# A new head and small moves in a turn of an attention kernel, with 74 products on TensorE that nobody reads

## What is computed

```python
# layer 0, per image: xf is (C, N)
q, k, v = Wq @ xf + bq, Wk @ xf + bk, Wv @ xf + bv      # q, k of 32 rows, v of 256
attn = softmax(q.T @ k, axis=-1)
x1 = gamma * (v @ attn.T) + xf
# layer 1
h = group_norm(x1, 32 groups, eps=1e-5)                  # with weight and bias per channel
q, k, v = q_w @ h + q_b, k_w @ h + k_b, v_w @ h + v_b   # all of 256 rows
attn = softmax(q.T @ k / 16, axis=-1)
y = x1 + proj_w @ (v @ attn.T) + proj_b
```

## Time and profile before

| | us |
|---|---|
| median of three runs | 840.06 |
| lowest and highest | 836.66, 841.46 |
| the profiled execution | 842.42 |
| its span | 840.6 |
| PE busy | 789.0 (94%) |
| DVE busy | 556.8 (66%) |
| ACT busy | 471.2 (56%) |
| POOL busy | 166.7 (20%) |
| mean granted clock of TensorE | 0.982 |

### The profile page before, as it was taken

The page is one execution under the profiler, slowest core; times in us unless marked ns, Lnnn a source line. Parts: engine busy times, 40 slices in busy tenths (PEclk is TensorE's granted clock), DMA queues, the critical chain, the costliest instruction groups (busy, mean ns, idle before and its releaser), DMA issues.

```text
span 840.6 us, 9682 instructions
## 1 busy us (share of the span) xinstructions
PE 789.0 (94%) x3756; PEld 645.5 (77%) x3756; DVE 556.8 (66%) x787; ACT 471.2 (56%) x609; POOL 166.7 (20%) x141
## 2 busy tenths in 40 slices
PE   5788887999999989999999999999999999999998
PEld 4567666888788777877778877888778788888786
DVE  5554675677758686676956777586865857385665
ACT  4755663557654576445854657545765457444343
POOL 3600233201310041103310034100421024102300
PEclk9879999899999999999999999999999999999999
DMA  7000001001100011000200002000100001000101
GB/s 225 0 1 2 1 0 51 1 1 40 62 1 1 1 51 51 1 1 1 83 19 1 1 0 101 1 1 1 50 1 1 2 1 50 1 1 1 50 1 51
DMA packets 10365, 18.98 MB, mean 23 GB/s; under 512 B 2128, under 2 KB 3920, under 8 KB 10320
## 3 DMA queue, kind: packets, MB, share of 16 engines
q1 hardware_dynamic: 10320, 18.36, 6.3%
HBM read 9.97 MB, written 8.39 MB: 22 GB/s over the span
## 4 chain that ended last, share of the span: by engine, by line
PE 70%; DVE 20%; ACT 7%; issue 2%; DMA 1%; SPq 0%; ACTq 0%; DVEq 0%
PE ring L524 22%; PE ring L526 21%; PE ring L525 21%; PE ring L534 3%; DVE pt_lo L946 3%; PE ring L544 2%; ACT prob L743 2%; DVE neg_raw L931 2%; DVE bn L989 2%; DVE x_lo L861 2%; DVE neg_max L929 2%; DVE pt_lo L949 1%; DVE h_lo L869 1%; ACT ring L764 1%; DVE res L982 1%
## 5 line engine op out<-in xcount | busy, mean ns | idle before, releaser
L524 PE MATMUL ring<-pt_hi,v_hi 128*128 128x512 f32 x512 | 204.1, 399 | 4.2 <-issue 2.0
L525 PE MATMUL ring<-pt_lo,v_hi 128*128 128x512 f32 x512 | 202.6, 396 | 0.0
L526 PE MATMUL ring<-pt_hi,v_lo 128*128 128x512 f32 x512 | 202.5, 395 | 0.0
L743 ACT ACTIVATE prob<-ring,neg_max 128x1024 f32<-128x1024 f32 x64 | 71.6, 1118 | 179.1 <-DVE neg_max L932 179.1
L931 DVE TENSOR_REDUCE neg_raw<-ring 128x1 f32<-128x1024 f32 x64 | 77.9, 1217 | 86.9 <-PE ring L526 86.9
L465 POOL TENSOR_TENSOR v_lo<-v_f,v_hi 128x512 fp32r<-128x512 f32 x32 | 42.9, 1341 | 440.8 <-ACT v_hi L781 440.8
L524 PEld LDWEIGHTS ring<-pt_hi,v_hi 128*128 128x128 f32 x512 | 97.5, 190 | 26.7 <-issue 3.8
L526 PEld LDWEIGHTS ring<-pt_hi,v_lo 128*128 128x128 f32 x512 | 97.6, 191 | 21.8
L525 PEld LDWEIGHTS ring<-pt_lo,v_hi 128*128 128x128 f32 x512 | 97.8, 191 | 19.3
L524 PE MATMUL ring<-h_hi,query_hi 128*128 128x512 f32 x256 | 101.2, 395 | 5.2 <-DVE spread L967 4.9
L929 DVE TENSOR_REDUCE neg_max<-ring 128x1 f32<-128x1024 f32 x64 | 77.7, 1221 | 42.0 <-PE ring L534 42.0
(11 more groups left out here) (118 smaller groups left out, 1234.5 us busy)
## 6 DMA issues: line engine op xcount, KB each, us to landing
...
```

Of the source, the lines that this page charges most:

```text
L524: mm(out, w_hi, m_hi, start=first, stop=False)
L525: mm(out, w_hi, m_lo, start=False, stop=False)
L526: return mm(out, w_lo, m_hi, start=False, stop=last)
L743: activation(prob[:, p % PROBS], ring[:, slot], ACT.Exp, bias=neg_max[:, k % 2:k % 2 + 1], accum_out=row_sum[:, k % 2:k % 2 + 1]).then_inc ...
```

## The change

1. **Products that nobody reads.** `keep_busy` multiplies a 128 x 128 float32 matrix of ones by itself into a place that is filled afresh later: 48 times at the very start (after the ones are there), 10 times ahead of the first keys tile, 16 times ahead of the first value product. 74 in all.
2. **New head.** The scores of image 0 are no longer broken up by the last two value projections, which come later. POOL splits the first two (ACT copies them to `v1_f` first), ahead of its split of image 1, which goes to `h_hi` and `h_lo` and waits for nothing of TensorE. DVE instead of ACT takes the weight products. A step "opening" gives ACT and DVE an order of their own for both projections of image 1 and the shift. The bias products move from step 5 to step 0 of the keys, beside value projection 2.
3. **Image 0's steps.** Scores of image 1 are `late` in every step instead of `early`; all keys go to one slot. The split of x of image 2 moves forward into steps 6 and 7, and its lo half from POOL to DVE.
4. **Image 1.** Statistics, both norms and the hidden rows a step later, with other hosts; both phases of layer 0 of images 0 and 1 are evacuated at once.
5. **A turn.** The first qk projection is late in step 0; in step 3 the second stands ahead of all banks; norms are in sides instead of late.

The diff, cut to its core:

```diff
-PLACE = {("qk", 1, 0): 0, ("qk", 1, 1): 3}
+PLACE = {("qk", 1, 0): 2, ("value0", 0, 2): 3, ("value0", 0, 3): 0, ("value0", 1, 0): 0, ("value0", 1, 1): 0}
...
-HOST = {("norm", 0, m): ("qk", 2, m) for m in range(2)}
+HOST = {("qk", 1, 1): ("qk", 1, 0), ("bias", 0, 0): ("value0", 0, 2),
+        ("norm", 0, 0): ("qk", 2, 1), ("norm", 0, 1): ("value0", 2, 0)}
...
 def first_image():
...
-    steps = [Step(slots=(0, 1, 2, 3)) for _ in range(2)]
-    steps += [Step(slots=(0, 1, 2)), Step()]
-    steps[0].sides = tiles("qk", 0, (0, 1)) + tiles("value0", 0, (0, 1))
-    steps[1].late = tiles("scores", 0, (0, 1, 2)) + tiles("value0", 0, (2,))
-    steps[1].late += tiles("scores", 0, (3,)) + tiles("value0", 0, (3,)) + tiles("scores", 0, (4,))
-    for m, k in enumerate((5, 6, 7)):
-        steps[2].late += tiles("weights", 0, (m,)) + tiles("scores", 0, (k,))
-    steps[2].log = steps[2].shifts = 0
-    steps[2].late += tiles("weights", 0, (3,))
-    steps[2].take_weights = True
-    steps[3].sides = tiles("qk", 1, (0,))
-    steps[3].late = tiles("shift", 0, (0,))
-    for k in range(TILES + 2):
-        step = Step(("keys", 0, k) if k < TILES else None, (0, 0, k - 2) if k >= 2 else None, 1)
-        if k == 0:
-            step.sides = tiles("qk", 1, (1,))
-        if k == 2:
-            step.late = tiles("scores", 1, (0,))
-        if 3 <= k <= 5:
-            step.early = tiles("scores", 1, (k - 2,))
-        if 6 <= k <= 8:
-            step.early = tiles("scores", 1, (k - 1,))
-        if k in (4, 6):
-            step.sides = tiles("value0", 1, (k // 2 - 2,))
-        steps.append(step)
-    steps[4 + 5].sides = tiles("bias", 0, (0,))
-    steps[4 + 5].late = tiles("scores", 1, (4,))
-    steps[4 + 8].early_log = 1
-    steps[4 + 8].sides = tiles("value0", 1, (2,))
-    steps[4 + 8].late = tiles("shift", 1, (0,))
-    steps[4 + 9].sides = tiles("keys", 1, (0,))
-    steps[4 + 9].late = tiles("value0", 1, (3,))
-    steps.append(Step(("keys", 1, 1)))
-    steps[-1].split_x = 2
-    return steps
+    start, scores, opening = Step(slots=(0, 1, 2, 3)), Step(slots=(0, 1, 2)), Step()
+    start.sides = tiles("qk", 0, (0, 1)) + tiles("value0", 0, (0, 1))
+    scores.late = tiles("scores", 0, (0, 1, 2))
+    for m in range(4):
+        scores.late += tiles("weights", 0, (m,)) + tiles("scores", 0, (3 + m,))
+    scores.late += tiles("scores", 0, (7,))
+    scores.take_weights = True
+    opening.opening = True
+    opening.sides = tiles("qk", 1, (0, 1)) + tiles("value0", 0, (2,))
+    opening.late = tiles("shift", 0, (0,))
+    steps = [Step(("keys", 0, k), (0, 0, k - 2) if k >= 2 else None) for k in range(TILES)]
+    steps[0].sides = tiles("bias", 0, (0,))
+    steps[0].rest = True
+    for k in range(7):
+        steps[k + 1].late = tiles("scores", 1, (k,))
+    steps[3].sides = tiles("value0", 0, (3,))
+    steps[4].sides = tiles("value0", 1, (0,))
+    steps[6].sides = tiles("value0", 1, (1,))
+    steps[6].split_x = steps[7].split_x_lo = 2
+    s8, s9, s10 = Step(None, (0, 0, 6)), Step(None, (0, 0, 7)), Step(("keys", 1, 1))
+    s8.early = tiles("scores", 1, (7,))
+    s8.early_log = 1
+    s8.late = tiles("value0", 1, (2,))
+    s9.sides = tiles("shift", 1, (0,))
+    s9.late = tiles("keys", 1, (0,)) + tiles("value0", 1, (3,))
+    return [start, scores, opening] + steps + [s8, s9, s10]
...
-    s3.statistics = 0
+    s4.statistics = 0
     s4.sides = tiles("qk", 2, (0,))
-    s4.late = tiles("norm", 0, (0,))
-    s5.sides = tiles("qk", 2, (1,))
-    s5.late = tiles("norm", 0, (1,))
+    s5.sides = tiles("qk", 2, (1,)) + tiles("norm", 0, (0,))
     s6.early = tiles("scores", 2, (0,))
-    s6.sides = tiles("value0", 2, (0,))
-    s6.hidden = s6.hidden_lo = 0
+    s6.sides = tiles("value0", 2, (0,)) + tiles("norm", 0, (1,))
+    s7.hidden = s7.hidden_lo = 0
...
     if has(i + 1):
-        steps[0].sides = tiles("qk", i + 1, (0,))
+        steps[0].late = tiles("qk", i + 1, (0,))
+        steps[3].banks_first = 0
         steps[3].sides = tiles("qk", i + 1, (1,))
...
         for m, s in enumerate((12, 13)):
-            steps[s].late = tiles("norm", i, (m,)) + steps[s].late
+            steps[s].sides += tiles("norm", i, (m,))
...
         if _k == TILES - 1:
-            if _layer == 0:
+            if _layer == 0 and _image >= 2:
                 STEPS[_n + 1].evacuate = (_layer, _image)
             else:
                 _step.evacuate_at_once = (_layer, _image)
...
+
+            return (h_hi, h_lo) if i == 1 else (x_hi, x_lo)
...
+            def first_values0():
+
+                for m in range(2):
+                    two = slice(2 * m, 2 * m + 2)
+                    pool.wait_ge(S["value0_taken"], m + 1)
+                    link(G.tensor_copy(v0_hi[:, two], v1_f[:, m]))
+                    G.tensor_tensor(v0_lo[:, two], v1_f[:, m], v0_hi[:, two].bitcast(F32),
+                                    ALU.subtract).then_inc(S["value0_first"], 1)
...
             small_things()
+            first_values0()
+            first_split_x()
+            bias_rows()
             pool.wait_ge(S["x0_loaded"], 16)
             pool.wait_ge(x_loaded[0], x_loads(0))
             residual0(0)
-            first_split_x()
-            bias_rows()
             split_weights()
-            split_x(2)
...
+            def keep_busy(out, passes):
+
+                for _ in range(passes):
+                    mm(out[:, 0:P], ones[:], ones[:], start=True, stop=True)
...
+            wait("ones_ready", 1)
+            keep_busy(ring[:, 3], 48)
             for now in STEPS:
-                if now.tile:
+                if now.tile == ("keys", 0, 0):
+                    wait_read(BEFORE[now.tile])
+                    keep_busy(ring[:, SLOT[now.tile]], 10)
+                if now.values == (0, 0, 0):
+                    fill(now.tile)
+                    wait_read(BEFORE[0, 0, 2])
+                    keep_busy(pv_ps[:, 0], 16)
+                elif now.tile:
                     fill(now.tile)
...
+                    got = out[:, 0:HALF].rearrange("p (j n) -> p j n", j=2)
+                    if i == 0 and m < 2:
+                        copy(v1_f[:, m], got).then_inc(S["value0_taken"], 1)
+                    else:
+                        copy(v0_hi[:, 2 * m:2 * m + 2], got).then_inc(S["value0_hi"], 1)
...
+            def opening():
+                log_sums(0)
+                for m in range(2):
+                    query_part(("qk", 1, m))
+                shift_rows(("shift", 0, 0))
+                key_part(("qk", 1, 0))
...
+                if now.rest:
+                    key_part(("qk", 1, 1))
+                    project_hi(("value0", 0, 2))
...
+            def take_weights():
+
+                dve.wait_ge(S["ring_ready"], RING_NO["weights", 0, 3] + 1)
+                wqq_ps, wpv_ps = weight_places(SLOT["weights", 0, 3])
+                V.tensor_scalar(wqq_f, wqq_ps, scale, None, ALU.mult).then_inc(S["weights_read"], 1)
+                V.tensor_copy(wpv_f, wpv_ps).then_inc(S["weights_read"], 1)
+
+            def opening():
+                key_part(("qk", 1, 0))
+                shifts(0)
+                key_part(("qk", 1, 1))
+                for m in range(2):
+                    query_part(("qk", 1, m))
...
+                if now.rest:
+                    project_lo(("value0", 0, 2))
+                    project_lo(("bias", 0, 0))
```

135 lines of the change are left out of this document (74 added, 61 removed).

## The result

| | before | changed |
|---|---|---|
| median of the runs beside each other | 840.76 us (836.66 to 841.80, 4 runs) | 849.54 us (847.36 to 849.95, 4 runs) |
| the profiled execution, its span | 842.42 us, 840.6 | 847.36 us, 845.6 |
| the same in a later session (the last experiment) | 841.4 us (23 runs) | 848.86 us (6 runs) |
| TensorE busy in the span | 94% | 95% |

The changed kernel takes 1.0093 times as long, 95% interval 1.0063 to 1.0124, and in the second session 1.0103, 1.0075 to 1.013. It is slower by some 8 us, outside the predicted range. Of the 8.8 us between the medians the two profiled executions show 4.9: the one of before is the slowest of its first five runs, the changed one the fastest of its own.

What follows compares the result with a forecast made beforehand. TensorE, busy 94%, bounds the kernel, with a head where PE, ScalarE and VectorE take turns. Terms -0.2 + 2.8 - 3.3 - 6.2 + 4.1 + 3.0 = +0.2 on 842.42 give 842.6, or 840 us against the median; range 830 to 847.

Steps and rivals of the forecast that it cites:

- The 48 products and the first scores: Head: products end at 13.7 us (14.7 if the clock rises late), first scores at 20.1 instead of 16.65, loss 3.5.
- Rival A: Head: products at half price end before 8.86 us, head 4.8 + 1.1 us earlier, about 834 us; chance 0.14.
- gain 0.2: Scores of image 0: first keys at 36.3 us against 36.54, the new order's nearly 5 us taken by the products.
- the shift (0.6): End of image 0's scores: DVE's shift operations, after weight products and two key rows, take 0.6 us.
- loss 2.8: Rest of image 0, up to keys (1,2): these start at 98.1 us, where before it was 95.49.
- The loop of ScalarE and VectorE: Image 0's key steps: exponents, hi, lo and maximum close a loop of 5.7 us a step; PE isn't the limit.
- exp(3): Image 0's loop: ScalarE's exponent of keys 3, predicted at 52.4 us; PE waits for it at the value projection.
- The 16 products ... I cost at nothing: Ahead of the first value product, 42.5 to 46.1 us: covered by a later wait, cost nothing; up to 3.6 otherwise.
- loss 3 (0 to 6): PE's idle stretches between 50 and 120 us: two to three clock falls on the chain, some 1.3 us each.
- gains of 3.3 and 6.2: Image 1: first query projection 33.4 us after keys (1,2) instead of 36.7; at-once evacuation brings first logits 6.2 earlier.
- loss 4.1: Steady turns: DVE idles 0.8 us more in each of 5 turns, PE's wait moving to keys 2 for q.
- Rival C: Image 0, steps 2 to 7: ACT and DVE's exchange bounds, with a cold PE inside; about 847 us; chance 0.16.

Runs made afterwards that it cites:

- e10: e8 plus the 48 unread products ahead of everything, in the old head: 839.84 us, ratio 0.9981 to the kernel before.
- e8: Kernel before with only layer 0 of images 0 and 1 evacuated at once: 835.2 us, ratio 0.9925 to the kernel before.
- e5: Changed kernel with the turn's moves undone and GpSimd's residual0(0) and split_weights behind the shift: 842.07 us, ratio 0.9995 to the kernel before.
- e6: e5 without the 48 products during the loads: 838.8 us, ratio 0.9959 to the kernel before.
- e3: Changed kernel with GpSimd starting residual0(0) and split_weights only after VectorE's shift pair is written: 844.72 us, ratio 1.004 to the kernel before.
- e15: Changed kernel without any edit, timed again beside the kernel before: 848.86 us, ratio 1.0103.
- e11: e5 without any of the 74 unread products: 836.35 us, ratio 0.994 to the kernel before.
- e7: e5 without the 16 products ahead of the first value product: 841.56 us, ratio 0.9995 to the kernel before.
- e14: e5 without the 10 products ahead of the first keys: 841.49 us, ratio 1.0015 to the kernel before.
- e4: Kernel before with the turn's moves alone: 845.51 us, ratio 1.0042 to the kernel before.
- e12: Kernel before with the turn's moves except the group sums, which stay where they were: 845.92 us, ratio 1.0053 to the kernel before.
- e2: Changed kernel with the turn's moves undone, head, products and evacuation kept: 844.05 us, ratio 1.0031 to the kernel before.

## Why the prediction was wrong

Its structure held nearly everywhere; the time came out wrong by terms that were missing or set to nothing. Point by point:

- **The 48 products and the first scores.** Predicted to end at 13.7, with the scores at 20.1; measured 13.58 and 19.87. Right in this profile; in the second they end at 14.71 and the scores come at 21.00, which is the late rise of the prediction's bound (14.7), for which it had no row. Alone they cost 4.7 us (e10 over e8) and 3.0 us (e5 over e6), against a predicted net of 3.5. Rival A, half the price, is out: the 20 records from 36.53 to the keys at 38.74 start 0.11 us apart, so a product takes 0.22, as counted. The Trainium skill (TensorE: Matmul & The Clock Gate, "Wait — 56ns, not 53.3ns?") gives 55.6 ns at full clock for 128 columns; one record of a float32 product takes twice that here, and there are two.
- **First keys, "gain 0.2": wrong by 2.4.** The step that failed is "the shift (0.6)" in the part on the scores of image 0. VectorE's three operations took 2.9 us, since residual0(0) and split_weights of GpSimd had been moved to just this place. I followed VectorE's, ScalarE's and TensorE's queues, didn't follow GpSimd's past this place, and took the 0.17 us from a moment in which GpSimd idled. Without the overlap the first keys came at 36.36 (e3), against a predicted 36.3, and the whole was 4.5 to 5.3 us faster: 2.4 directly, the rest by the clock in that profile. In the second profile (e15) the first keys are 5.2 us later than predicted: 0.9 up to the first scores, 2.7 up to the shift, and 1.6 because the 10 products ran at a low clock.
- **The rest of image 0, "loss 2.8".** The loop of ScalarE and VectorE is right: in e11, without products, the value projection of step 3 starts 17.2 us behind the first keys (32.35 to 49.53), and the prediction's exp(3) ended 17.2 us behind them. From that projection to keys (1,2) the prediction has 44.6 us and e3 shows 44.4. "The 16 products ... I cost at nothing" held only where they ran at full clock. In e5 they take 3.74 us, near the predicted 3.6, and the distance of 17.2 us is the same with them as without them in e7. In the changed kernel they take 5.37 us, with a clock of 0.56 from 45.0 to 48.0 us, and the distance is 18.45 (in e3 4.73 and 18.3). They delay the scores behind them, which the loop needs. So this term was short by 1.3 us, and the clock made it so.
- **The clock, "loss 3 (0 to 6)".** About right, but it isn't one number. The last stretch took 44.4 us in e3 and e14, 46.0 in e5, 47.1 in the changed kernel and 47.5 in e11: 2.7 us in the changed kernel. In image 1 the first query projection came 34.5 us behind keys (1,2) (104.33 to 138.85), against a predicted 33.4; but it took 34.1 us in e5 too, at a clock of 1.00. So 0.4 of these 1.1 us are the clock's, and 0.7 were counted too short.
- **Image 1 and the evacuation, gains of 3.3 and 6.2.** Predicted 47.1 us from keys (1,2) to the first logits, measured 48.45 (48.1 in e5 at a clock of 1.00), before 56.64. The evacuation alone gave 6.3 (e8). Right but for 1.3 us: the 1.1 just named and 0.2 behind the first query projection.
- **The turns, "loss 4.1".** 0.82 us a turn, with the waits named and VectorE idle for 0.77 where 0.8 was predicted; 3.5 and 4.5 us in e4 and e12. Right.

In the profiled executions the misses (2.4 for the shift, 1.3 for the 16 products, 0.7 in image 1, 0.1 of clock) add up to 4.5 of the 4.8 us by which 847.36 exceeds the 842.6 of the sum. The rest of the distance to the medians is the spread of the head that e15 shows, and that the medians of before, 840.06 and 840.76, lay low in a kernel whose runs go from 836.8 to 843.2 in the last session. That the clock's 3 us came out so close is in part luck: in e3 and e14 the last stretch lost nothing.

One reading ahead of the sum was off, with no term resting on it: the page's digits are almost all 9 from slice 8 on, not from slice 6, and slice 7 reads 7. Rival C, at 847, had the right sign and a part of the mechanism (a cold TensorE in image 0, the 16 products uncovered), but not the cause in the head.

The parts add up. In distances of ratios times 842: turn +3.5 to 4.5, evacuation -6.3, the 48 products +3.0 to 4.7, the 10 and 16 together +1.6, GpSimd beside the shift +3.0 (e2 to e5) to 5.3 (e3), the new order itself +1.3 (e11 over e8). The sum is 6.1 to 11.1, the change measured 7.8 and 8.7. It is a weaker test than it looks: the steps from e15 over e2, e5, e6, e11 and e8 to the kernel before form a chain whose differences add up by construction. The turn in e4 and e12, the 48 products in e10 and the evacuation in e8 were measured by themselves in the old kernel.

What stays open is why the clock falls behind one wait of 3.6 us and not behind another of the same length, and why the 16 products ran at full clock in e5 and in part at the low one elsewhere. A turn with the projection late but ahead of lo(keys 0) on VectorE wasn't tried.
